# Second attention of a two-block transformer kernel: probability counts transposed by DMA instead of TensorE, exponent bias on GpSimd

## What is computed

```python
q = (x @ Wq + bq).reshape(1, B * N, H, hd)          # 1024 queries, 16 heads of 32
kv = (cond @ Wkv + bkv).reshape(1, -1, 2, H, hd)    # 2048 keys and values
q = _fq_sym(q * scale); k = _fq_sym(k); v = _fq_sym(v, axis=2)   # to 8-bit steps
attn = softmax(einsum('bhqd,bhkd->bhqk', q, k))     # per head 1024 x 2048
attn = _fq_unsigned(attn, axis=-1)                  # round(255 * p / max p), a count 0..255
out = einsum('bhqk,bhkd->bhqd', attn, v) @ Wp + bp
```

## Time and profile before

| | |
|---|---|
| runs | 1842.77 us median of 3 (1842.15 to 1843.25) |
| profiled execution | 1850.55 us, its span on the core 1848.9 us |
| TensorE busy, share of the span | 81% |
| VectorE | 61% |
| ScalarE | 49% |
| GpSimd | 20% |
| granted TensorE clock, mean | 0.931 of full speed |

### The profile page before, as it was taken

One profiled execution on the slowest core, in us unless ns is written; L12 is line 12 of the kernel. 1 busy time (PEld: TensorE's weight loads), 2 busy tenths in 40 slices (PEclk: granted clock), 3 DMA queues, 4 the chain that ended last, 5 costly groups with the idle time before them and its releaser, 6 DMA issues.

```text
span 1848.9 us, 28384 instructions
## 1 busy us (share of the span) xinstructions
PE 1489.4 (81%) x9982; PEld 835.9 (45%) x10040; DVE 1119.0 (61%) x1941; ACT 902.4 (49%) x1195; POOL 370.5 (20%) x179
## 2 busy tenths in 40 slices
PE   6887088888885389999999999386888888788878
PEld 3443055555553334444444444143555545454434
DVE  5778789899988201111111111376999999995565
ACT  3445278788785101111111111035888888893853
POOL 1001000000000346899970000311000000000150
PEclk9988589999998589999999999787999999999998
DMA  5547311121110499999998885352000000000101
GB/s 181 176 147 225 133 46 60 60 75 60 60 72 11 157 372 385 371 375 400 401 384 307 307 306 212 97 187 68 25 16 26 26 26 26 13 14 2 67 1 46
DMA packets 102753, 273.85 MB, mean 148 GB/s; under 512 B 7208, under 2 KB 11304, under 8 KB 101680
## 3 DMA queue, kind: packets, MB, share of 16 engines
q1 hardware_dynamic: 87904, 223.65, 33.0%
q0 software_dynamic: 10816, 40.90, 7.0%
q10 hardware_dynamic: 3984, 8.65, 1.2%
HBM read 212.62 MB, written 38.27 MB: 136 GB/s over the span
## 4 chain that ended last, share of the span: by engine, by line
PE 44%; DVE 32%; issue 12%; ACT 4%; DMA 3%; POOL 2%; SPq 1%; DVEq 1%; POOLq 0%; ACTq 0%
PE scores L863 17%; DVE arena L1626 13%; PE bank L879 9%; DVE arena L1431 6%; DVE arena L1445 3%; DMA arena<-in_ctx 2%; PE scores L690 2%; PE bank L777 2%; PE bank L1069 2%; PE bank L1001 1%; PE bank L871 1%; PE bank L908 1%; PE bank L761 1%; DVE arena L1632 1%; POOL arena L629 1%
## 5 line engine op out<-in xcount | busy, mean ns | idle before, releaser
L1626 DVE TENSOR_SCALAR_CACHE_REDUCE arena<-scores,arena 128x1024 f32<-128x1024 f32 x256 | 318.0, 1280 | 20.9 <-PE scores L924 17.6
L863 PE MATMUL scores<-arena 128*128 128x512 f32 x736 | 321.8, 595 | 0.8 <-DVE arena L1563 0.8
L1571 DVE TENSOR_TENSOR arena<-scores,arena 128x512 f32<-128x512 f32 x46 | 31.8, 692 | 447.3 <-PE scores L863 447.3
L1225 ACT ACTIVATE arena<-arena 128x2048 int16<-128x2048 f32 x128 | 255.8, 1999 | 59.1 <-DVE arena L1632 58.8
L924 PE MATMUL scores<-arena 96*128 96x512 bf16 x512 | 159.8, 399 | 77.0 <-DVE arena L1626 66.3
L863 PEld LDWEIGHTS scores<-arena 128*128 128x128 f32 x736 | 140.6, 191 | 178.0 <-issue 176.9
L879 PE MATMUL bank<-arena 128*128 128x512 f32 x368 | 163.3, 597 | 3.6 <-issue 3.4
L941 PE MATMUL bank<-arena 128*128 128x128 f32 x1024 | 142.4, 284 | 8.2 <-ACT arena L1235 2.9
L1193 ACT ACTIVATE arena<-scores 128x512 f32<-128x512 f32 x46 | 27.5, 597 | 248.8 <-PE scores L863 248.8
L941 PEld LDWEIGHTS bank<-arena 128*128 128x128 f32 x1024 | 116.7, 145 | 62.5 <-issue 36.1
L1160 ACT ACTIVATE arena<-bank 128x512 f32<-128x512 f32 (+3 forms) x256 | 118.0, 511 | 48.1 <-PE bank L761 36.4
(11 more groups left out here) (238 smaller groups left out, 2461.2 us busy)
## 6 DMA issues: line engine op xcount, KB each, us to landing
arena<-in_L_ffn_w SPq DMA_DIRECT2D x69, 2048.0 KB, 12.5
arena<-arena SPq DMA_DIRECT2D x64, 260.0 KB, 2.3
kst_d<-arena POOLq DMA_DIRECT2D x16, 384.0 KB, 6.4
tern_d<-arena POOLq DMA_DIRECT2D x12, 512.0 KB, 7.1
arena<-tern_d SPq DMA_DIRECT2D x3, 2048.0 KB, 10.7
arena<-kst_d SPq DMA_DIRECT2D x16, 384.0 KB, 3.6
xs_d<-arena SPq DMA_DIRECT2D x23, 256.0 KB, 3.3
arena<-xs_d SPq DMA_DIRECT2D x23, 256.0 KB, 13.8
```

Source lines behind the costliest of these rows:

```text
L863: ins = pe.matmul(scores[:, m * 1024 + half * 512:m * 1024 + half * 512 + 512], xsT[a][:, c], wa[:, m, c, half * 512:half * 512 + 512], st ...
L1225: act.activation(p16[i], ssb[i], ACT.Exp, bias=ebias[i], scale=-1.0, accum_out=rsum[a][:, t:t + 1]).then_inc(p_ready, 1)
L1626: dve.tensor_scalar(ssb[i][:, s:s + 1024], scores[:, s:s + 1024], nsq[:, bass.ds(h, 1), t], None, ALU.mult, ALU.min, accum_out=nmx[i][:, h ...
```

## The change

For every tile one DMA, issued by SyncE, transposes the 128 x 2048 counts of `p16` as 16-bit elements from SBUF to SBUF, into 16 blocks of 128 keys x 128 queries (`pT`, now with 16-bit elements). The 8 TensorE transposes of a tile, ScalarE's copy and VectorE's copy are gone, and with them banks 4 and 5 from the stage. `p16` and `pT` have four buffers each instead of two; two of each lie where `xn3` lay. In step t TensorE now issues the scores of tile t + 2 and the product of tile t - 3 (LAG = 3), and VectorE finishes the head before in step 4 instead of 2. Values are loaded in their own order instead of pair by pair. The bias is formed on GpSimd, in order, tile by tile; the copy of the next head's values comes after the bias of tile 5. SyncE's queue loads head h + 2 after the transpose of the last tile of head h. Some semaphores are merged (`zero_made` into `consts_made`; `vmax_ready` and `wsum_all` into `all_reduced`), which changes no instruction besides.

```diff
-PAIRS = NC // 2
-LOW = PAIRS // 2
+PBUF = 4
+LAG = 3
...
-        p16 = [rq.take(I16, B * SK) for _ in range(2)]
-        pT = [rq.take(I32, PAIRS, P) for _ in range(2)]
+        over_xn3 = Region(base, base + 4 * NT * D)
+        p16 = [r.take(I16, B * SK) for r in (rq, rq, over_xn3, over_xn3)]
+        pT = [r.take(F16, NC, P) for r in (rq, rq, over_xn3, over_xn3)]
...
@@ sync
-            sweep(sp, H, load_head)
+            load_head(0)
+            load_head(1)
+            for n in range(H * NT):
+                i = n % PBUF
+                if n >= PBUF:
+                    sp.wait_ge(av_done, n - PBUF + 1)
+                sp.wait_ge(p_ready, n + 1)
+                sp.dma_start_transpose(pT[i], p16[i].bitcast(F16)).then_inc(pT_in[i], 16)
+                h, t = divmod(n, NT)
+                if t == NT - 1 and h + 2 < H:
+                    sp.wait_ge(s_done, 2 * NT * (h + 1))
+                    load_head(h + 2)
...
@@ gpsimd
-                pool.dma_start(vchunk[a].rearrange("j (c e) d -> j c (e d)", e=2),
-                               v_d[tiles].rearrange("t p d -> (t p) d").rearrange("(c j e) d -> j c (e d)", j=P, e=2)).then_inc(v_back, 16)
+                pool.dma_start(vchunk[a], v_d[tiles].rearrange("t p d -> p t d")).then_inc(v_back, 16)
...
-            sweep(pool, H, stage_v)
+            def make_bias(h, t):
+                i, n = t % 2, 8 * h + t
+                pool.wait_ge(s_read, 2 * n + 2)
+                pool.tensor_scalar(ebias[i], nmx[i][:, 0:1], nmx[i][:, 1:2], LN255, ALU.min, ALU.add).then_inc(bias_ready, 1)
+
+            def bias_head(h):
+                for t in range(NT):
+                    make_bias(h, t)
+                    if t == LAG + 2 and 0 < h < H - 1:
+                        pool.wait_ge(av_done, 8 * h)
+                        stage_v(h + 1, (h + 1) % 2)
+            stage_v(0, 0)
+            stage_v(1, 1)
+            for h in range(H):
+                bias_head(h)
...
@@ tensor
-            def a1_turn(h, a, t, first):
...
             def a1_pv(h, a, t, first):
-                i = t % 2
+                i = t % PBUF
-                if t % 2 == 0:
-                    pe.wait_ge(pT_lo, 4 * h + t // 2 + 1)
-                pe.wait_ge(pT_hi, 8 * h + t + 1)
+                pe.wait_ge(pT_in[i], 16 * (2 * h + t // PBUF + 1))
...
-                    ins = pe.matmul(bank[:, t * HD:(t + 1) * HD], both[:, c // 2, c % 2], vhead[a][:, c], start=c == 0, stop=c == NC - 1)
+                    ins = pe.matmul(bank[:, t * HD:(t + 1) * HD], pT[i][:, c], vhead[a][:, c], start=c == 0, stop=c == NC - 1)
...
-                    a1_turn(h, a, t, first and t == 0)
-                    if t > 0:
-                        a1_pv(h, a, t - 1, first)
+                    if t >= LAG:
+                        a1_pv(h, a, t - LAG, first)
                     elif not first:
-                        a1_pv(h - 1, 1 - a, NT - 1, False)
+                        a1_pv(h - 1, 1 - a, t - LAG + NT, False)
...
@@ scalar
-                if not (first and t < 2):
-                    act.wait_ge(p_turned, 2 * n - 2)
+                if not (first and t < PBUF):
+                    act.wait_ge(pT_in[t % PBUF], 16 * (2 * h + t // PBUF))
...
-                    act.wait_ge(p_turned, 2 * (8 * h + t) + 2)
-                    c = 0 if t % 2 else LOW
-                    act.activation(pT[t % 2][:, c:PAIRS].rearrange("p c n -> p (c n)"), bank45[:, c * P:PAIRS * P].bitcast(I32), ACT.Copy).then_inc(pT_hi, 1)
...
@@ vector
-                    if t % 2 == 0:
-                        dve.wait_ge(p_turned, 2 * (8 * h + t) + 1)
-                        dve.tensor_copy(pT[t % 2][:, 0:LOW].rearrange("p c n -> p (c n)"), bank45[:, 0:LOW * P].bitcast(I32)).then_inc(pT_lo, 1)
-                    if t < NT - 2:
-                        make_bias(h, t + 2)
-                    elif not last:
-                        make_bias(h + 1, t + 2 - NT)
-                    if t == 2 and not first:
+                    if t == LAG + 1 and not first:
                         finish_head(h - 1, 1 - a)
```

More of the change, by code:

```diff
@@ L199, in program @@
         ones_set = sem("ones_set")
-        v_step, vmax_ready, v_stored, v_back, v_made = (
-            sem(n) for n in ("v_step", "vmax_ready", "v_stored", "v_back", "v_made"))
+        v_step, all_reduced, v_stored, v_back, v_made = (
+            sem(n) for n in ("v_step", "all_reduced", "v_stored", "v_back", "v_made"))
         rk = Region(base)
@@ L381, in program @@
         s_done, s_read, bias_ready = sem("s_done"), sem("s_read"), sem("bias_ready")
-        p_ready, p_turned, pT_lo, pT_hi = (sem(n) for n in ("p_ready", "p_turned", "pT_lo", "pT_hi"))
+        p_ready = sem("p_ready")
+        pT_in = [sem(f"pT_in{i}") for i in range(PBUF)]
         av_done, a_post = sem("av_done"), sem("a_post")
@@ L387, in program @@
         wpiece_loaded = [sem(f"wpiece_loaded{a}") for a in range(2)]
-        wpiece_done, wsum_done, wsum_all, w_mean = (sem(n) for n in ("wpiece_done", "wsum_done", "wsum_all", "w_mean"))
+        wpiece_done, wsum_done, w_mean = (sem(n) for n in ("wpiece_done", "wsum_done", "w_mean"))
         w_in = [sem(f"w_in{a}") for a in range(2)]
@@ L430, in _ @@
                 store_v(u)
-            sp.wait_ge(zero_made, 1)
+            sp.wait_ge(consts_made, CONSTS + 1)
             for s in range(SLOTS):
@@ L495, in _, with load_head @@
                 sp.wait_ge(kst_stored[a], 16 * (NC // 2))
[L497 to L501, removed]
-            sweep(sp, H, load_head)
+            def load_head(h):
+                a = h % 2
+                sp.dma_start(khead[a][0:K3, :], kst_d[h]).then_inc(k_loaded[a], 16)
+                sp.dma_start(qhead[a][0:K3, :], qst_d[h]).then_inc(k_loaded[a], 16)
+            load_head(0)
[10 more added lines that the diff above has]
+                    load_head(h + 2)
             sp.wait_ge(o_added, 2 * NT)
@@ L966, in a1_head @@
                         a1_scores(h + 1, 1 - a, t + 2 - NT, False)
-                    a1_turn(h, a, t, first and t == 0)
-                    if t > 0:
-                        a1_pv(h, a, t - 1, first)
+                    if t >= LAG:
+                        a1_pv(h, a, t - LAG, first)
                     elif not first:
-                        a1_pv(h - 1, 1 - a, NT - 1, False)
+                        a1_pv(h - 1, 1 - a, t - LAG + NT, False)
                 if last:
-                    a1_pv(h, a, NT - 1, False)
+                    for t in range(NT - LAG, NT):
+                        a1_pv(h, a, t, False)
             pe.wait_ge(qf_done, NT)
@@ L1134, in _ @@
             std(1)
-            act.wait_ge(vmax_ready, 1)
+            act.wait_ge(all_reduced, 1)
             for b in range(B):
@@ L1224, in exp_tile @@
                 act.wait_ge(bias_ready, n + 1)
-                act.activation(p16[i], ssb[i], ACT.Exp, bias=ebias[i], scale=-1.0, accum_out=rsum[a][:, t:t + 1]).then_inc(p_ready, 1)
+                act.activation(p16[t % PBUF], ssb[i], ACT.Exp, bias=ebias[i], scale=-1.0, accum_out=rsum[a][:, t:t + 1]).then_inc(p_ready, 1)
             def a1_head(h, a, k, first, last):
```

32 lines of the change are left out of this document (11 added, 21 removed).

## The result

| | median, us | range of the runs | profiled execution | its span |
|---|---|---|---|---|
| before | 1842.68 (4 runs) | 1842.15 to 1843.25 | 1850.55 | 1848.9 |
| changed | 1812.53 (4 runs) | 1807.69 to 1814.0 | 1807.69 | 1806.1 |

The ratio is 0.9832, with a 95% interval of 0.9812 to 0.9852. The changed kernel is 30 us faster. The forecast was 1922 us, some 80 us slower. The range held the time; the sign was wrong.

The account below looks back on a forecast made before the run. VectorE bounds the old kernel, SyncE's queue the changed one: 128 x 3.63 = 464.6 us, 12.6 for loads, then landing 2.3 and product 0.57, stage 79 us longer; 1922 us against 1842.77, range 1780 to 1990.

Parts of the forecast that it names:

- What bounds the kernel: Second attention before the change: VectorE sets the pace, working 388 of 408 us, with ScalarE and TensorE not far behind.
- The bias on GpSimd: Second attention, between read and exponential: the bias takes 0.30 us on GpSimd, plus 0.39 for two hops.
- the ring: Two `ssb` buffers: read, bias, exponential, then read of tile n + 2; 5.37 us per turn, 2.68 per tile.
- rival 1: Second attention: SyncE's queue keeps up at under 2.7 us per transpose, the ring bounds; 1787 us, chance 0.38.
- The transposes on SyncE's queue: All 128 issued one behind another, 128 pieces of 4 KB each at 28 ns: 3.58 us, and 0.05 to the next.
- the cheap end: Issue of one transpose on SyncE's queue at the lower price, 20.6 ns per share: 2.64 us.
- the dear end: Issue of one transpose on SyncE's queue at the SBUF to SBUF price, 31.7 ns per share: 4.06 us; total 1983.
- The engines' own work is hidden under it: The 16 DMA engines need 2.1 us for a transpose's 512 KB, hidden under its issue on SyncE's queue.
- Its own signs: For rival 1: short transposes, SyncE waiting for the counts, reads following one another with gaps under 0.3 us.
- Landing: Issue to landing of a transpose: 2.3 us by the copies in the sum, about 3.5 in rival 1.
- Rival 2's clock: Second attention: TensorE falls to 1.2 GHz, 3.0 us per tile, 1828 us; rival 2 as a whole has chance 0.06.
- Head loads: A head's two loads hold SyncE's queue 0.90 us between transposes; fourteen heads, 12.6 us.

Follow-up runs that it names:

- `half_transpose`: Changed kernel with each DMA transpose cut to the first 1024 of 2048 keys, the second half's counts left out; 1794.33 us, ratio 0.9734 to before.
- `two_loads`: Changed kernel without loads of keys and queries of heads 2 to 15, which use those of heads 0 and 1; 1799.49 us, ratio 0.9739 to before.
- `split_12_4`: Changed kernel with 12 of 16 key blocks turned by DMA, the rest in pairs by TensorE and copied by ScalarE; 1796.65 us, ratio 0.9731 to before.
- the free-running stretch: Kernel before plus 128 unread 128 x 2048 DMA transposes, paced only by four destination buffers, later head loads behind them; 2135.5 us.
- `four_split_8_8`: Changed kernel with 8 of 16 key blocks turned by DMA, 8 by TensorE, and four buffers for scores, bias and maxima; 1781.73 us, ratio 0.9667 to before.
- `four_split_12_4`: Changed kernel with 12 of 16 key blocks turned by DMA, 4 by TensorE, and four buffers for scores, bias and maxima; 1797.9 us, ratio 0.9738 to before.

## Why the prediction was wrong

**What bounds the kernel: right.** The pace was VectorE's, and taking the copy and the bias from it gave the gain. (One reading was wrong: the earlier trace rows has VectorE at 9 tenths in four early slices too, not only from the 28th on.) But I did not ask what the bias alone would bring. The experiment on it gives 29.4 of the 35 us, with VectorE still the fullest engine.

**The bias on GpSimd: right.** 0.30 us taken, 0.29 measured. 5.37 us for a turn of the ring, 5.28 measured. But the sum of rival 1 left the finish out of the ring: 2.68 us per tile taken, 2.73 measured with the finish where nothing else binds (`half_transpose`, `two_loads`), which is 6 us over the stage. The two reads, the exponential and the finish kept their lengths beside the transposes.

**The transposes on SyncE's queue: the step that failed.** "The largest pieces seen are 4 KB ... I take 28 ns: 3.58 us." The issue took 1.67 us at the least and 1.99 in the middle, below even the cheap end of 2.64. The price per piece came from dividing copies of 0.33 and 0.51 us by 16, although has the same 0.34 us for 384 and for 192 KB, so nothing in those rows grew with size. Two sizes of transpose show the split: at the least 1.23 us for 64 pieces of 4 KB, 1.67 for 128, so 6.9 ns per piece and 0.8 fixed. (1.41 for 96 in `split_12_4` lies within 0.04 us of that line.) I had named the fixed part as the reason for not taking the dear end, and then kept 28 ns.

The Trainium skill, "DMA: Bandwidth & Descriptors", in its passage on the accelerated HWDGE path, gives 262,144 cycles for 8,192 tiles for the generations before, 32 per tile. With the 1.2 GHz that the Trainium skill, "Advanced Engine Details and Errata", "Clock Domains", gives for SyncE, 6.9 ns are an estimated 8 cycles. So the trace does not agree, if a tile is a piece of 4 KB as the forecast read it; what a tile is there, no run here shows.

**"The engines' own work is hidden under it ... 2.1 us": the second error.** It was the bound, at 2.52 us. The pieces were not 4 KB either. The page's count of packets, changed kernel:

```profile
DMA packets 368990, 340.91 MB, mean 189 GB/s; under 512 B 273448, under 2 KB 277544, under 8 KB 367920
```

The kernel before has 102,753, of which 7,208 under 512 bytes. The difference, 266,240 small ones, is 2080 per transpose, about 252 bytes each, the size of a row of 128 two-byte counts. On 16 engines 2.52 us are 19.4 ns for each.

The Trainium skill, "Advanced Engine Details and Errata", "X-Bar Transpose (TRN2)", expects 350 to 400 GB/s of transposing DMAs. The trace does not agree: 512 KB in 2.52 us are 208 GB/s, and the free-running stretch shows 209. The rule pointed to the right sign all the same, and I gave it no more than rival 1's 0.38.

**Rival 1 had the sign**, and half of the mechanism: a transpose cost the queue under 2.7 us and the ring was near. Its own signs did not come, since SyncE did not wait for the counts; the forecast's picture of an unbroken queue did, with transposes of 2.4 us in the middle instead of 3.6. The forecast's last sign, wrong at its root if the queue needs under 3.0 us, is what happened. Rival 1 gave 1787 where 1812.5 was measured. Its stage was 349.9 us against 370.8; 15.6 of the 21 lie in the reads: 6 are the finish that its ring left out, less what the turn was shorter, 9 the DMA engines above the ring (358.6 against 349.5). The other 5.3 are the tail, for which I had 6.9. It took 12.2, because transposes still stood in line when the last read ended. The last products wait for one landing after the other:

```profile
1616.39 1.28 DVE L1624 TENSOR_SCALAR_CACHE_REDUCE arena<-scores,arena 128x1024 f32<-128x1024 f32 x1
...
1620.37 0.61 PE L959 MATMUL bank<-arena 128*128 128x32 bf16 x16 [2.04 <-DMA arena<-arena]
...
1629.23 0.61 PE L959 MATMUL bank<-arena 128*128 128x32 bf16 x16 [3.24 <-DMA arena<-arena]
```

**Landing:** 2.3 us taken in the sum and 3.5 in rival 1, 4.7 measured, 3.1 for half the bytes. **Rival 2's clock** came true, a granted clock of 0.50 all through, but its price did not: the two halves of scores take 1.03 us each, so 2.1 of the 2.8 us a tile has, and the product's 0.6 lies mostly beside the reads. **Head loads:** 0.90 us per head in the queue was counted, with its gaps; 1.2 to 1.8 measured, mostly 1.4, and their bytes cost more, some 2.0.

**Open:** why the start of the stage moves by up to 17 us between kernels that are alike up to it, and how much of the gain of `four_split_8_8` over `four_split_12_4` is the clock's.

## What to carry to other kernels

Before a long price is put on an operation that no row shows, split the nearest rows into a fixed part and a part per byte; a price per piece that carries the fixed part is several times too dear when multiplied by 128. A transfer has two prices, its issue on the queue and its packets on the engines, and each must be set beside the pace of the loop, with everything else that moves there. When a change has two parts, price each alone: here the small one held most of the gain, and the large one did best, of the three shares tried, with half the work.

## What the runs showed of the hardware

- A transpose by DMA of 128 x 2048 two-byte values, SBUF to SBUF, takes 2.52 us of all 16 engines (208 GB/s), 1.42 us with 1024 columns; issued alone it holds the queue for at least 1.67 and 1.23 us, and behind others for up to 4.7.
- The packets' busy share is no share of time once they stand in line: it read 1.12 at 211 GB/s in the changed kernel, and 0.64 at 121 GB/s with half the bytes.
- A DMA share of 0.99 (189 GB/s) beside the kernel before disturbed no other engine: reads 1.28 us and exponentials 2.00, with 128 idle transposes as without.
- TensorE was granted 0.50 through a stage in which the page calls it busy 260 of 300 us, with 1.03 us in place of 0.59 for a half of the scores; with four turns of a constant more per tile it was granted 0.94.
